# The last attention's scores: three products of rounded parts over zero-padded queries, or one plain fp32 product per head on half of the array's rows

## What is computed

```python
xn = layernorm(x) * ln_g + ln_b
q = split_heads(xn @ Wq)              # 16 heads of 64
kv = xn @ Wkv                         # own keys and values: 100 rows
mem = split_heads(ctx_1024 @ Wm)      # 722 rows, keys and values alike
k = concatenate([k, mem]); v = concatenate([v, mem])     # 822 rows
attn = softmax(einsum('bhid,bhjd->bhij', q, k) * 64 ** -0.5)
out = einsum('bhij,bhjd->bhid', attn, v) @ Wo + bo
```

## Time and profile before

| | us |
|---|---|
| median of 3 runs | 1920.87 |
| lowest and highest run | 1920.75, 1921.82 |
| span of the profiled execution, first to last instruction | 1915.0 |
| PE busy in it | 1695.5 (89%) |
| DVE, ACT, POOL busy | 1117.1, 794.7, 142.9 |

### The profile page before, as it was taken

The page is one execution under the profiler, slowest core; times in us unless marked ns, Lnnn a source line. Parts: engine busy times, 40 slices in busy tenths (PEclk is TensorE's granted clock), DMA queues, the critical chain, the costliest instruction groups (busy, mean ns, idle before and its releaser), DMA issues. The chain is left out here.

```text
span 1915.0 us, 31965 instructions
## 1 busy us (share of the span) xinstructions
PE 1695.5 (89%) x11552; PEld 1430.1 (75%) x11552; DVE 1117.1 (58%) x1856; ACT 794.7 (42%) x1416; POOL 142.9 (7%) x189
## 2 busy tenths in 40 slices
PE   6996359999999589889999999999999709999993
PEld 5775359999999289568787878778787609999981
DVE  5765546667677553125555556565557436766765
ACT  2443135555555143124444444344445215445440
POOL 4000310000000301100000000000000040000004
PEclk9998579999999789889999999999999759999997
DMA  9300265655666346241212111121111055665644
GB/s 343 132 9 1 82 231 201 212 202 197 209 208 219 97 176 240 71 115 36 57 29 52 39 47 39 42 53 30 44 23 23 1 202 180 217 213 188 217 144 123
DMA packets 117458, 236.62 MB, mean 124 GB/s; under 512 B 54232, under 2 KB 74840, under 8 KB 102268
## 3 DMA queue, kind: packets, MB, share of 16 engines
q1 hardware_dynamic: 100396, 182.28, 29.9%
q0 software_dynamic: 16976, 53.11, 8.0%
HBM read 187.17 MB, written 48.17 MB: 123 GB/s over the span
## 5 line engine op out<-in xcount | busy, mean ns | idle before, releaser
L955 DVE TENSOR_TENSOR e_lo<-e_raw,e_hi 128x2048 fp32r<-128x2048 f32 x118 | 270.4, 2291 | 129.0 <-ACT e_hi L1018 129.0
L918 PE MATMUL banks<-e_xh,e_hi 128*128 128x256 f32 x1024 | 291.8, 285 | 12.3 <-DVE e_xl L971 7.4
L918 PE MATMUL banks<-e_xh,e_lo 128*128 128x256 f32 x1024 | 291.1, 284 | 0.0
L918 PE MATMUL banks<-e_xl,e_hi 128*128 128x256 f32 x1024 | 291.1, 284 | 0.0
L1600 PE MATMUL banks<-a_wm,a_ch 128*128 128x512 f32 (+1 forms) x768 | 250.1, 407 | 13.5 <-DVE a_cl L1736 13.5
L1018 ACT CAST e_hi<-e_raw 128x2048 fp32r<-128x2048 f32 x118 | 224.7, 1904 | 70.5 <-PE banks L935 28.6
L918 PEld LDWEIGHTS banks<-e_xh,e_hi 128*128 128x128 f32 x1024 | 197.4, 193 | 20.7 <-issue 8.2
L918 PEld LDWEIGHTS banks<-e_xl,e_hi 128*128 128x128 f32 x1024 | 197.3, 193 | 5.6
L918 PEld LDWEIGHTS banks<-e_xh,e_lo 128*128 128x128 f32 x1024 | 197.2, 193 | 0.0
L1634 PE MATMUL banks<-a_kT,a_qD 128*100 128x512 f32 (+1 forms) x768 | 173.9, 362 | 1.9 <-DVE a_kT L1746 1.9
L1752 DVE TENSOR_REDUCE a_nmax<-banks 100x1 f32<-100x822 f32 x128 | 129.5, 1012 | 75.7 <-PE banks L1634 75.7
(11 more groups left out here) (237 smaller groups left out, 2742.4 us busy)
## 6 DMA issues: line engine op xcount, KB each, us to landing
e_raw<-wout SPq DMA_DIRECT2D x50, 1024.0 KB, 4.7
e_raw<-w SPq DMA_DIRECT2D x34, 1024.0 KB
e_raw<-wgate SPq DMA_DIRECT2D x17, 1024.0 KB
e_raw<-wup SPq DMA_DIRECT2D x17, 1024.0 KB, 4.8
a_craw<-ctxT SPq DMA_DIRECT2D x40, 256.0 KB, 2.9
e_xs<-slot_rows SPq DMA_DIRECT2D x18, 512.0 KB
slot_outs<-e_y POOLq DMA_DIRECT2D x16, 512.0 KB, 3.2
slot_rows<-a_zero POOLq DMA_DIRECT2D x15, 512.0 KB, 10.4
```

The source lines that it names most:

```text
L918: mm = nc.tensor.matmul(ps[:, bank, 0:CAP], w[:, cc, cut], x[:, cc, :], start=t == 0, stop=t == len(terms) - 1)
L955: nc.vector.tensor_tensor(lo[g % 2][i][:], raw[q % RAW][:], hi[g % 2][i][:].bitcast(F32), ALU.subtract)\
```

## The change

Four things change in the last attention.

1. Queries and keys are no longer split. `project` stages one fp32 tile, `p_stage`: ACT copies chunks 0 and 2, DVE chunks 1 and 3, and POOL stores it with one transfer in place of two. `own_q` and `own_k` are half as large.
2. `attend` loads one query tile `a1_q` (one transfer, no zeroed copies, no clearing by POOL) and one key tile. The six transposes of the keys are copied out once, in parallel: ACT takes 512 columns, DVE 210.
3. The scores of both heads are made in one call, in plain fp32: head 0 from partitions 0 to 63 and head 1 from partitions 64 to 127, alternating, two key halves each. There are four matmuls where twelve stood.
4. The order on the engines follows. DVE does both maxima, then the keys' copy, then both normalisations; ACT does both exponentials in a row. On PE, what stands between the two `turn` calls is no longer `scores(p, m, 1)` but `attended`, the second values product or the output product.

```diff
-        qD = [k.sb(c, f"a1_qD{u}", [128, 2, 2, T], F32R) for u in range(SLOTS)]
-        kT = [k.sb(c, f"a1_kT{u}", [128, 2, KEYS], F32R) for u in range(SLOTS)]
+        q = [k.sb(c, f"a1_q{u}", [128, T]) for u in range(SLOTS)]
+        kT = [k.sb(c, f"a1_kT{u}", [128, KEYS]) for u in range(SLOTS)]
...
+    def between(m, left):
+
+        return "output" if m == 1 else "values" if left >= 1 and m in END else "attended"
...
-                def scores(p, m, two):
+                def scores(p, m):
                     s = m % SLOTS
-                    after(pe, ex, 2 * p + two - 1)
+                    after(pe, ex, 2 * p)
                     for f, (first, wide) in enumerate(WIDE):
-                        for t, (q, kk) in enumerate(((0, 0), (0, 1), (1, 0))):
-                            mm = nc.tensor.matmul(ps[0:T, 2 * two + f, 0:wide], qD[s][:, q, two, :],
-                                                  kT[s][:, kk, first:first + wide], start=t == 0, stop=t == 2)
+                        for two in range(2):
+                            r = slice(HD1 * two, HD1 * two + HD1)
+                            mm = nc.tensor.matmul(ps[0:T, 2 * two + f, 0:wide], q[s][r, :],
+                                                  kT[s][r, first:first + wide], start=True, stop=True)
...
                 def step(b, u, m, left):
                     p = IC * b + m
                     if left >= 0:
-                        scores(p, m, 0)
+                        pe.wait_ge(k_a, p + 1)
+                        pe.wait_ge(k_v, p + 1)
+                        scores(p, m)
...
+                    if what != "attended":
+                        heads()
                     if left >= 1 and m in MIDDLE:
                         values_ahead(b, MIDDLE[m])
                     if exists(p - 1):
                         if ahead:
-                            pe.wait_ge(tl, p + 2)
+                            pe.wait_ge(k_a, p + 2)
+                            pe.wait_ge(k_v, p + 2)
                         turn(p - 1, (m - 1) % IC, 0)
-                    if left >= 0:
-                        scores(p, m, 1)
+                    if what == "attended":
+                        heads()
+                    elif what == "values":
+                        values_ahead(b, END[m])
+                    elif exists(p - 2):
+                        output(b, left)
                     if exists(p - 1):
                         turn(p - 1, (m - 1) % IC, 1)
-                    if left >= 1 and m in END:
-                        values_ahead(b, END[m])
...
                 def keys(p, m):
-                    s = m % SLOTS
-                    dve.wait_ge(th, p + 1)
-                    nc.vector.tensor_tensor(kT[s][:, 1, T:KEYS], two_banks(4)[:, 0:S],
-                                            kT[s][:, 0, T:KEYS].bitcast(F32), ALU.subtract).then_inc(tl, 1)
+                    dve.wait_ge(tk, p + 1)
+                    nc.vector.tensor_copy(kT[m % SLOTS][:, T + 512:KEYS], ps[:, 5, 0:S - 512]).then_inc(k_v, 1)
...
                         highest(p, m, 0)
+                        highest(p, m, 1)
                     if left >= (1 if m == IC - 1 else 0):
                         keys(p + 1, (m + 1) % IC)
-                    if exists(p - 1):
-                        normalise(p - 1, (m - 1) % IC, 1)
                     if left >= 0:
                         normalise(p, m, 0)
+                        normalise(p, m, 1)
                     if left >= 1 and m in MIDDLE:
                         evacuate(b + 1, 1 - u, MIDDLE[m], 6)
                     if exists(p - 1):
                         turned(p - 1, (m - 1) % IC, 0)
-                    if left >= 0:
-                        highest(p, m, 1)
+                    if left >= 1 and m in END:
+                        evacuate(b + 1, 1 - u, END[m], 6)
                     if exists(p - 1):
                         turned(p - 1, (m - 1) % IC, 1)
-                    if left >= 1 and m in END:
-                        evacuate(b + 1, 1 - u, END[m], 6)
...
-                    nc.scalar.copy(kT[m % SLOTS][:, 0, T:KEYS], two_banks(4)[:, 0:S]).then_inc(th, 1)
+                    nc.scalar.copy(kT[m % SLOTS][:, T:T + 512], ps[:, 4, :]).then_inc(k_a, 1)
```

More of the change, by code:

```diff
@@ L1584, in _ @@
                 over_steps(sp, step)
-            @block.gpsimd
-            def _(pool):
-                for s in range(SLOTS):
-                    pool.memset(qD[s][:].bitcast(U32), 0).then_inc(made, 1)
             @block.tensor
@@ L1674, in step, with heads @@
                             keys(p + 1, m + 1, u)
-                    if exists(p - 2):
-                        ub = u if m >= 2 else 1 - u
-                        if m == 2:
-                            pe.wait_ge(v_in[u], 8 * (b - u) + 16)
-                        attended(p - 2, (m - 2) % IC, ub)
+                    what = between(m, left)
+                    def heads():
+                        if exists(p - 2):
+                            if m == 2:
+                                pe.wait_ge(v_in[u], 8 * (b - u) + 16)
+                            attended(p - 2, (m - 2) % IC, u if m >= 2 else 1 - u)
+                    if what != "attended":
+                        heads()
                     if left >= 1 and m in MIDDLE:
@@ L1844, in step @@
                         exponent(p, m, 0)
-                    if exists(p - 2):
+                        exponent(p, m, 1)
+                    what = between(m, left)
+                    if exists(p - 2) and what != "attended":
                         attended(p - 2, (m - 2) % IC)
@@ L1850, in step @@
                         turned(p - 1, (m - 1) % IC, 0)
+                    if exists(p - 2) and what == "attended":
+                        attended(p - 2, (m - 2) % IC)
+                    if what == "values":
+                        evacuate(b + 1, 1 - u, END[m], 6)
+                    if exists(p - 1):
                         turned(p - 1, (m - 1) % IC, 1)
-                    if left >= 0:
-                        exponent(p, m, 1)
-                    if left >= 1 and m in END:
-                        evacuate(b + 1, 1 - u, END[m], 6)
                     if m in SPLIT and left >= SPLIT[m][0]:
```

91 lines of the change are left out of this document (42 added, 49 removed).

## The result

| | before | changed | |
|---|---|---|---|
| time, median (7 runs each) | 1919.86 us | 1913.55 us (1911.18 to 1915.17) | ratio 0.9968, 95% interval 0.9958 to 0.9978 |
| span of the profiled execution | 1915.0 us | 1911.9 us | -3.1 us |

The change saves 0.3%, 6.3 us, where 11 were forecast (1910 us, 0.62 on faster). The sum hides several misses that cancel. This table divides the profiled span by the start of PE's matmuls: A from the first values product of `attend` to the first scores, B the 56 steps of the first seven batches, C the seven steps up to the last pair's scores, D from there to the first matmul of `route`, E from there to the end. Ahead of A lie 807.3 us before and 806.7 us in the changed kernel.

The account below looks back on a forecast made before the run. PE's instruction stream was taken to bound 56 of 64 steps; -36 (steps) + 21 (waits given back) + 5 (last batch) - 1 (first keys) = -11 us, from the median 1920.87 to 1910 us, range 1888 to 1928.

Parts of the forecast that it names:

- The scores' price: Scores slot on PE in each step: both heads' four fp32 matmuls side by side take 1.38 + 0.16 = 1.54 us.
- The likeness to attended: Attended's two fp32 column tiles run wholly side by side, 0.16 us for mode changes; row tiles were taken to do the same.
- no overlap: Rival for the scores slot: row tiles run one after the other, slot 2.9 us, +88 us, 1999 us; chance 0.10.
- one record late: Rival for the scores: records start strictly in program order, at least 1.81 us, +27 us, 1938 us; chance 0.08.
- The steps: 56 steps of the first seven batches: 0.64 us gained in each, -36 us, against +21 us of new waits.
- Step 2: Step after the output step: DVE is late, so PE waits 1.75 us for bank 6's copy in place of 0.4.
- The last batch: No values product covers waits: 6.9 us per step for 6.14, five steps +3.8, step 2 +1.3, sum +5 us.
- POOL's clearing: nothing: Start of attend: dropping the clearing gains nothing, since 45 us of values products come before the first scores.
- SP ...: nothing: SP's queue: two transfers per pair in place of three, three pairs ahead with DMA nearly idle, gain nothing.
- The end of the stage: From the last pair's scores to the first matmul of route: forecast change 0 us.

Follow-up runs that it names:

- e3: Kernel before, with the first three context loads moved to the head of SP's queue; no arithmetic touched: 1913.27 us, ratio 0.9966 to the kernel before.
- e1: Changed kernel with the scores matmuls over all 128 partitions, so no row tiles (heads not separated): 1974.84 us, ratio 1.0284 to the kernel before.
- e2: Changed kernel with the scores matmuls reordered, both key halves of head 0 first, then head 1: 1911.55 us, ratio 0.9954 to the kernel before.
- e6: Changed kernel with the output step's context split and DVE's first addition to x ahead of the second turned copy: 1905.81 us, ratio 0.9923.
- e5: Changed kernel with attended, and ACT's copy of it, moved behind the first values product in steps 2, 3 and 4: 1900.91 us, ratio 0.9896.
- e7: Changed kernel with DVE's copy of the keys placed between its two maxima, in all batches: 1911.11 us, ratio 0.9952 to the kernel before.
- e4: Changed kernel with the old head of SP's queue: wait for POOL's clearing and extra own loads ahead of the context loads: 1917.35 us, ratio 0.9984.
- e9: Changed kernel with attended moved, output step and last batch reordered, ACT copying attended before the second exponential in its output step: 1879.82 us, ratio 0.9796.
- e8: Changed kernel, keys' copy between maxima; in the last batch first turned copies ahead of the second normalisation (DVE) and exponential (ACT): 1903.03 us, ratio 0.9913.

## Why the prediction was right, and where it was wrong

The time lies in the stated range and the change is faster, as forecast. That it came out faster is luck. The sum had the steps 6 us too good and the end of the stage 6 us too good; what made up for it is a gain of 6.4 us at the start of the stage which had been costed at nothing. Against e3, which has that gain without the change, the change is worth nothing that the medians show. In the working itself 19.4 should be 19.5 and 1999 be 1998, and nothing hangs on either. The mechanism of the steps was read rightly, that of the start was not.

- **The scores' price: right.** 1.54 us forecast, 1.56 measured. The likeness to attended, two tiles wholly side by side, carried the decision, and e1 shows what it was worth: 2.77 us without it. The rivals "no overlap" and "one record late" are out, the latter by e2.
- **The steps: right in kind, 6 us too hopeful.** -15 was forecast for B, -9.1 came. In steps 3 and 4 the forecast was -0.65 + 0.40 = -0.25 us each, and they gained 0.05 and 0.01: the wait was 0.48, the keys' transposes ahead of attended cost 0.77 against 0.71, the values products 0.01 to 0.05 more, and the second turn 0.70 against 0.54. Plain steps gained 0.53 to 0.61, not 0.64, since their turns cost 0.69 and 0.74. Each is under 0.2 us, but they recur in 56 steps.
- **Step 2: right.** A turn slot 1.5 us longer against the 1.75 forecast, by the very chain that was counted; e6 removed it by that chain. The output step came out 0.56 worse than forecast and step 2 0.5 better: the output product's last record had run beside the next scores, and now takes its full 0.43 us (slot 6.92 in place of 6.46), while in step 2 scores of 1.52, not 1.12, went.
- **The last batch: right in its steps, by luck in its sum.** 6.85 us forecast as 6.9, five times +0.7. Step 2 was forecast at +1.3. It cost 0.6 us where it ran at full clock (e5: 7.55 us against 6.92 before), and 1.6 more in the changed kernel's profile at the lower clock, a term that the sum did not have. So C is +5.7 in this profile and +4.1 in e5's, against +5. Its two waits came out at about 0.1 over and 0.2 under what was worked out: the turn started 2.44 us after the key transposes' start (1472.20 to 1474.64; 2.35 was worked out), and the second wait, put at 0.3, was under 0.1 (attended's slot 1.44 in place of 1.36) until e7 took the first away.
- **"POOL's clearing: nothing" and "SP ...: nothing": the step that failed.** The working was that the values products cover the own loads until the first scores. So they do; but behind those loads in SP's queue stood the context loads, which the values products themselves wait for. The trace of before showed it (ACT's idle of 10.41 us for the context, PE's gap, clock at 0.66), and I had read neither that stretch nor what is queued behind the moved issues. A came out 6.4 us shorter than forecast, as much as the whole gain in the median: e3 takes that gain with the kernel before and lands on the same time.
- **The end of the stage: not in the sum.** D rose by 5.9 us in this profile, by 3.1 to 3.2 in e2, e4, e5 and e7, whose code at the end is the changed kernel's or nearly so. These 3 us are gone in e9 (25.38), but the reordered copies took only 0.9 us by themselves (the wait for the first turned copy 2.22 us in e5, 1.29 in e9). The other 2.8 us between e5 and e9 are the clock: from that wait's end to the output product e5 takes 9.65 us and e9 6.88, with equal waits between, and e5's clock is at 0.50 for 6.8 us of it. The 2.7 us more in the changed kernel and e6 are the lower clock lasting 13.7 us and reaching into the output product (8.96 us in place of 7.11). Executions differ in this without any change of the code: e2, with the changed kernel's order, has 29.05. That the lower clock follows the idle PE fits each profile's order of events, but idle time alone doesn't decide it: e8 and e9 have the same three waits at the end (1.29, 0.76, 0.71), and only e8's clock fell there (for 3.4 us, D 26.93 in place of 25.38). What else decides is open.
- **E**, 400.4 to 402.6 us over all profiles, is code that no kernel here changes. The kernel before has the only one under 401.2, while e3, which has the same code there, has 402.12. So the +2.2 lies in that one execution rather than in the change. What lies ahead of A differs likewise, from 805.3 to 810.4 us.

Against e3, which has that gain without the change, the change is worth nothing that the medians show. In the working itself 19.4 should be 19.5 and 1999 be 1998, and nothing hangs on either. The mechanism of the steps was read rightly, that of the start was not.

- **The scores' price: right.** 1.54 us forecast, 1.56 measured. The likeness to attended, two tiles wholly side by side, carried the decision, and e1 shows what it was worth: 2.77 us without it. The rivals "no overlap" and "one record late" are out, the latter by e2.
- **The steps: right in kind, 6 us too hopeful.** -15 was forecast for B, -9.1 came. In steps 3 and 4 the forecast was -0.65 + 0.40 = -0.25 us each, and they gained 0.05 and 0.01: the wait was 0.48, the keys' transposes ahead of attended cost 0.77 against 0.71, the values products 0.01 to 0.05 more, and the second turn 0.70 against 0.54. Plain steps gained 0.53 to 0.61, not 0.64, since their turns cost 0.69 and 0.74. Each is under 0.2 us, but they recur in 56 steps.
- **Step 2: right.** A turn slot 1.5 us longer against the 1.75 forecast, by the very chain that was counted; e6 removed it by that chain. The output step came out 0.56 worse than forecast and step 2 0.5 better: the output product's last record had run beside the next scores, and now takes its full 0.43 us (slot 6.92 in place of 6.46), while in step 2 scores of 1.52, not 1.12, went.
- **The last batch: right in its steps, by luck in its sum.** 6.85 us forecast as 6.9, five times +0.7. Step 2 was forecast at +1.3. It cost 0.6 us where it ran at full clock (e5: 7.55 us against 6.92 before), and 1.6 more in the changed kernel's profile at the lower clock, a term that the sum did not have. So C is +5.7 in this profile and +4.1 in e5's, against +5. Its two waits came out at about 0.1 over and 0.2 under what was worked out: the turn started 2.44 us after the key transposes' start (1472.20 to 1474.64; 2.35 was worked out), and the second wait, put at 0.3, was under 0.1 (attended's slot 1.44 in place of 1.36) until e7 took the first away.
- **"POOL's clearing: nothing" and "SP ...: nothing": the step that failed.** The working was that the values products cover the own loads until the first scores. So they do; but behind those loads in SP's queue stood the context loads, which the values products themselves wait for. The trace of before showed it (ACT's idle of 10.41 us for the context, PE's gap, clock at 0.66), and I had read neither that stretch nor what is queued behind the moved issues. A came out 6.4 us shorter than forecast, as much as the whole gain in the median: e3 takes that gain with the kernel before and lands on the same time.
- **The end of the stage: not in the sum.** D rose by 5.9 us in this profile, by 3.1 to 3.2 in e2, e4, e5 and e7, whose code at the end is the changed kernel's or nearly so. Most of these 3 us go with the order of e8 and e9 (D 26.9 and 25.4): they were the waits behind both normalisations. The other 2.7 stand only in the profiles of the changed kernel and of e6. That the idle PE brings the lower clock is suggested by the order of the two in each profile; no run held the waits and kept the clock, so it is not shown.
- **E**, 400.4 to 402.6 us over all profiles, is code that no kernel here changes.

Against e3, which has the same start, the change itself gives 9.1 us in B, loses 5.7 in C and 3 to 6 in D: nothing that the medians could tell (1913.55 and 1913.27). e9 is built on it; whether e3's kernel would gain as much from a like reordering was not tried.

## What to carry to other kernels

- When a change shortens a queue's issues, read what stands behind them in that queue and who waits for it, at the first use of every buffer; the cover of the moved item says nothing of the items behind it. A cheap check is to issue the other loads first in the unchanged kernel.
- Work taken out between a product and the next one into the same bank takes its cover away too. Put independent work there (attended here), and keep the copies that free a bank ahead of work for which nobody waits yet.
- A stage's last iterations have no filler, so one order on the helper engines need not serve both. Removing one wait there shows the next (e7) until the chain is ordered as a whole (e8).

## What the runs showed of the hardware

- Two 64-row fp32 tiles that write different banks run side by side (eight records in a slot of 1.56 us, against 2.77 over all rows in e1), and each takes its matmuls independently of program order between them (e2: 14 ns between the starts). The pair of matmuls per head costs 1.38 us of records and a slot of 1.56.
- The fp32 output product ahead of the fp32 transposes has a slot of 6.92 us, and 6.46 ahead of the fp32r scores, where the last of its 16 records runs beside them. That the type decides, and not the size of what follows, was not tried apart.
- Granted clock: 0.66 over the 10 us that held PE's gap of 4.76 us in the kernel before, 1.00 there in e3 without the gap. In the changed kernel it fell to 0.50 at 1484.0 us, in a stretch (1482 to 1487) in which PE was busy 2.81 of 5 us.
- The same wait of 2.34 us came with the clock falling right behind it (changed kernel, step 2 of the last batch, +1.6 us) and without (e5). Over e6's six runs the mean granted clock goes from 0.938 in the shortest, 1900.02 us, to 0.931 in the longest, 1909.72. A difference of a few us between two kernels that idle at such places can be this alone.
